# One square per batch on ScalarE and one sum on VectorE for the Frobenius norms of the converted gradients

## What is computed

```python
def _zeropower_ns5(G):
    X = G.astype(jnp.bfloat16)
    ...
    nrm = jnp.linalg.norm(X.astype(jnp.float32).reshape(X.shape[0], -1), axis=1)
    X = X / (nrm[:, None, None].astype(jnp.bfloat16) + 1e-07)
    for a, b, c in NS_COEFFS:
        A = X @ jnp.swapaxes(X, 1, 2)
        Bm = b * A + c * (A @ A)
        X = a * X + Bm @ X
```

## Time and profile before

| what | value |
|---|---|
| time, median of 3 runs | 716.71 us (711.73, 716.71, 719.69) |
| the profiled execution's own time | 712.38 us |
| its span, first to last instruction | 710.6 us |
| mean granted clock of TensorE over it | 0.983 of full |
| busy share PE, DVE, ACT, POOL | 94%, 68%, 49%, 30% |

### The profile page before, as it was taken

One profiled execution on the slowest core, in us unless ns is written; L12 is line 12 of the kernel. 1 busy time (PEld: TensorE's weight loads), 2 busy tenths in 40 slices (PEclk: granted clock), 3 DMA queues, 4 the chain that ended last, 5 costly groups with the idle time before them and its releaser, 6 DMA issues.

```text
span 710.6 us, 11547 instructions
## 1 busy us (share of the span) xinstructions
PE 665.6 (94%) x4132; PEld 568.1 (80%) x4132; DVE 483.3 (68%) x960; ACT 345.2 (49%) x746; POOL 212.3 (30%) x210
## 2 busy tenths in 40 slices
PE   3998889779997899998999999999999999999997
PEld 3778779779995688887888888888888888888885
DVE  4788888999995478767545675665754766655555
ACT  3367669879998976453322323323223223223222
POOL 2255867944037664134100330013200331000000
PEclk9999999999998899999999999999999999999999
DMA  8000000021000000032003432243212432121223
GB/s 315 1 0 1 2 1 1 1 68 48 3 3 2 0 1 1 0 118 92 30 15 83 118 104 72 63 108 112 85 60 76 117 118 69 60 69 59 66 72 122
DMA packets 20472, 41.48 MB, mean 58 GB/s; under 512 B 3360, under 2 KB 3616, under 8 KB 20288
## 3 DMA queue, kind: packets, MB, share of 16 engines
q1 hardware_dynamic: 19392, 37.65, 17.2%
q10 hardware_dynamic: 832, 2.43, 1.0%
q0 software_dynamic: 192, 0.66, 0.2%
HBM read 38.50 MB, written 2.23 MB: 57 GB/s over the span
## 4 chain that ended last, share of the span: by engine, by line
PE 73%; ACT 9%; DVE 9%; POOL 3%; issue 3%; DMA 2%; ACTq 0%; DVEq 0%; POOLq 0%
PE ps L987 36%; PE ps L1058 18%; ACT junk L634 3%; PE ps L804 3%; PE ps L917 2%; PE ps L893 2%; PE ps L918 2%; PE ps L904 2%; PE ps L933 2%; DMA qkvw<-in_qkvw 1%; PE ps L834 1%; ACT junk L586 1%; PE ps L1005 1%; PE ps L1024 1%; DVE sq L1172 1%
## 5 line engine op out<-in xcount | busy, mean ns | idle before, releaser
L705 ACT ACTIVATE sgm<-ps,zero 128x512 f32<-128x512 f32 x100 | 68.9, 690 | 268.7 <-PE ps L987 268.7
L987 PE MATMUL ps<-h2hi,whi 128*128 128x512 f32 x400 | 156.1, 390 | 0.0
L987 PE MATMUL ps<-h2lo,whi 128*128 128x512 f32 x400 | 155.6, 389 | 0.0
L987 PE MATMUL ps<-h2hi,wlo 128*128 128x512 f32 x400 | 155.6, 389 | 0.0
L1466 DVE TENSOR_TENSOR am<-sgm,ps 128x512 f32<-128x512 f32 x88 | 60.6, 688 | 138.6 <-ACT sgm L705 138.5
L449 POOL CAST whi<-raw 128x768 fp32r<-128x768 f32 x25 | 22.4, 895 | 239.2 <-DMA raw<-in_moew 236.7
L987 PEld LDWEIGHTS ps<-h2lo,whi 128*128 128x128 f32 x400 | 75.1, 188 | 15.7
L987 PEld LDWEIGHTS ps<-h2hi,whi 128*128 128x128 f32 x400 | 75.1, 188 | 15.5
L987 PEld LDWEIGHTS ps<-h2hi,wlo 128*128 128x128 f32 x400 | 75.1, 188 | 15.4
L1058 PE MATMUL ps<-ahi,whi 128*128 128x512 f32 x200 | 77.9, 390 | 0.1
L1058 PE MATMUL ps<-alo,whi 128*128 128x512 f32 x200 | 77.8, 389 | 0.0
(11 more groups left out here) (206 smaller groups left out, 1238.5 us busy)
## 6 DMA issues: line engine op xcount, KB each, us to landing
raw<-in_moew SPq DMA_DIRECT2D x25, 384.0 KB, 3.8
cw<-combine SPq DMA_DIRECT2D x32, 256.0 KB, 3.2
cw<-combine SPq DMA_DIRECT2D x16, 224.0 KB, 3.0
cw<-combine SPq DMA_DIRECT2D x16, 192.0 KB, 2.9
cw<-combine SPq DMA_DIRECT2D x16, 160.0 KB, 2.7
cw<-combine SPq DMA_DIRECT2D x16, 128.0 KB, 3.0
out<-x1T SPq DMA_DIRECT2D x8, 256.0 KB, 3.7
cw<-combine SPq DMA_DIRECT2D x16, 96.0 KB, 2.8
```

Of the source, the lines that this page charges most:

```text
L705: ac.activation(sgm[:, n % 2, :], gate_bank(n), ACT.Silu, bias=zero[:, :]).then_inc(S["e_sg"], 1)
L987: last = mm(o, w_, a_[:, kc, tok], start=(kc == 0 and k == 0), stop=(kc == KC - 1 and k == 2))
```

## The change

The six activations of `grad_squares(b)` become one activation over all six matrices of the batch, 128x768 elements, without the running sum; it writes the squares to a new tile `xsq` in fp32, which lies in memory that the queries no longer need. A new DVE function `square_sums(b)` sums `xsq` along the rows into six columns of `fss`. It is called in DVE's pass b + 2 between the second `dgb` operation and `cast_grads`, for b = 0 to 5, and for b = 6 after the loop, between a copied transpose and `x_init(3)`. The semaphore `f_sq` says that the squares are there; `f_ss` now counts batches. Batch 7 is treated as before.

```diff
@@ memory and semaphores
         X = at("X", [P, NMAT, P], BF16, R_q)
+        xsq = at("xsq", [P, 6, P], F32, R_q + NMAT * P * 2)
...
-            "xb_ok", "f_ss", "g_sq", "f_s7",
+            "xb_ok", "f_sq", "f_ss", "g_sq", "f_s7",
@@ ScalarE
             def grad_squares(b):
                 ac.wait_ge(S["xb_ok"], b + 1)
-                for m in range(b * 6, b * 6 + 6):
-                    if m:
-                        ac.wait_ge(S["f_ss"], m)
-                    ac.activation(junk[:, :], X[:, m, :], ACT.Square, bias=zero[:, :], accum_out=fss[:, m:m + 1]).then_inc(S["f_ss"], 1)
+                if b:
+                    ac.wait_ge(S["f_ss"], b)
+                ac.activation(xsq[:, :, :], X[:, b * 6:b * 6 + 6, :], ACT.Square, bias=zero[:, :]).then_inc(S["f_sq"], 1)
@@ TensorE
             def frob_sums(b):
                 if b < B - 1:
-                    pe_.wait_ge(S["f_ss"], 6 * (b + 1))
+                    pe_.wait_ge(S["f_ss"], b + 1)
@@ VectorE
+            def square_sums(b):
+                ve.wait_ge(S["f_sq"], b + 1)
+                ve.tensor_reduce(fss[:, 6 * b:6 * b + 6], xsq[:, :, :], AX.X, ALU.add).then_inc(S["f_ss"], 1)
+
             for b in range(B):
...
                 ve.tensor_tensor(dgb[i][:, :, :], dgb[i][:, :, :], dh_ps(i), ALU.mult).then_inc(S["b_dg"], 1)
+                if b >= 2:
+                    square_sums(b - 2)
                 if b >= 1:
                     cast_grads(b - 1)
                 if b >= 5:
                     x_init(b - 5)
             first_turned(1)
+            square_sums(B - 2)
             x_init(B - 5)
             x_init(B - 4)
             x_init(B - 3)
```

## The result

The changed kernel takes 719.58 us (median of 20 runs, 715.12 to 722.31), the kernel before, measured beside it, 714.69 us (median of 20 runs, 709.70 to 719.69). The ratio is 1.0067 with a 95% interval of 1.0049 to 1.0086: slower by 4.8 us (3.5 to 6.1). The profiled execution took 720.61 us, its span 718.8.

A forecast was written before the change was run, and what follows sets the result against it. The prediction took PE and ACT as full in the gradient passes, with DVE close and leading into the rounds. 3.7 us to the first `Br` plus 0.6 for the clock gave +4.3 on 716.71: 721.0 us, range 715.5 to 726.0.

The forecast's parts named there:

- The sign and the size: Whole kernel: slower by 4.3 us, 0.6%, to 721.0 us; chance 0.55.
- What bounds the passes: Gradient passes: PE is full, so the 2.2 us a pass that ACT gives back only turns into waiting.
- The prices: New instructions: ACT's square of 128x768 takes 0.93 us, DVE's sum of 128x768 takes 0.953 us.
- DVE up to its last gradient operation: Passes 3 to 7: DVE's sums partly fill idle time, leaving the second `dgb` of pass 7 1.21 us late.
- The hand-over: Into the Newton-Schulz rounds: new waits make transposes 2.35 us later, `x_init(3)` 4.4 and the first `Br` 3.7.
- The clock: PE behind its second gap, 3.0 us long: the clock may fall, costing +0.6 us, bounds 0 and 1.4.
- That sums and GpSimd get in each other's way: Rival, passes 5 to 7: sums stretch by 0.5 us each beside GpSimd, +5.8 us, 722.5 us; chance 0.08.
- a net gain from ACT: Rival, gradient passes: DVE's sums stay hidden and ACT's relief counts, 715.7 us; chance 0.08.
- The last hand-over costs less: Rival, into the rounds: ACT is free earlier or DVE has unseen slack, about +2 us, 718.7 us; chance 0.16.
- A slowdown of over 1% by the clock: Rival, PE between 135 and 155 us: low clock stretches follow one another, +7.2 us, 723.9 us; chance 0.13.

The follow-up runs named there:

- The kernel without the hand-over's waits: Changed kernel, PE's batch 5 sum over partitions behind first transposes in another PSUM bank, DVE's batch 6 sum between two divisions: 47.09 us to `Br`, ratio 1.0040.
- the two that moved one of them each: Changed kernel with DVE's batch 6 sum behind three divisions, 47.94 us to `Br`; or PE's batch 5 sum over partitions behind first transposes, 48.42 us.
- the kernel whose first gap was filled: Changed kernel with 64 unused identity products on PE ahead of batch 5's sum over partitions: 48.05 us to `Br`, ratio 1.0038.

## Why the prediction was right, point by point

- **The sign and the size.** Forecast were +4.3 us, 0.6%; measured +4.8 (3.5 to 6.1), 0.67%. The predicted 721.0 us is 1.4 over the measured 719.58, since it was added to a median of three runs, 716.71, which twenty runs put at 714.69. The profiles account for 3.6 us, and for 0.9 more in one of two executions; what may be left up to 4.8 lies inside the interval, and no stretch shows it.
- **What bounds the passes.** Right in the main: taking 1.9 us a pass from ACT is worth 0.66 us in all. But the prediction put it at nothing, by reading PE's busy 5.83 of 5.88 us as full, and the pass without the sums took 5.53. A second thing was missed. PE waits for DVE's sums in the early passes too, 0.35 to 0.38 us each for batches 0, 2 and 3, besides the 1.40 for batch 4; the first made pass 3 0.25 us longer, of which pass 4 gave 0.12 back.
- **The prices.** ACT's square 0.93 us forecast, 0.927 measured; DVE's sum 0.953 forecast, 0.944 measured.
- **DVE up to its last gradient operation.** +1.21 forecast, +0.98 measured, and not by the forecast's steps: DVE was 0.23 us late by pass 4 already, where the forecast had nothing, behind PE's wait for the sum of batch 0. The sums do fill the idle time ahead of the casts. Further on, DVE's instructions beside GpSimd's took other times than before: the cast of pass 6 took 0.98 us for 0.55, `x_init(1)` 1.15 for 1.36, and the second gate operation of passes 6 and 7 0.69 for 0.97 and 0.96.
- **The hand-over.** The transposes +2.35 forecast and +2.36 measured, `x_init(3)` +4.4 and +4.40, `Br` +3.7 and +3.60. The first is right partly by luck: DVE was 0.2 us less late, and PE's sum over partitions, for which I took 0.27 us, took 0.42 in the slow clock. The kernel without the hand-over's waits (47.09) shows that the mechanism is the one named; the two that moved one of them each won less than expected.
- **The clock.** +0.6 forecast, between 0 and 1.4. It was +0.88 in one profile and nothing in the other; that a value between them came near the measured time is luck. The step that was off is the length of PE's second gap, 3.0 us forecast and 2.15 and 1.43 measured. PE came out of its first gap in the slow clock, which lasted some 6.8 us and not the 3.45 of before; the gradient products of batch 7 took 4.5 and 5.2 us, 3.9 before, and filled part of the second gap. With these products at 2.9 us, in the kernel whose first gap was filled, the second gap was 2.87.
- **The rivals.** That sums and GpSimd get in each other's way is out: 0.94 to 0.95 us for all seven. So is a net gain from ACT: the rival priced the relief at 0.96 us, alone it is worth 0.66, and DVE's sums cost more. "The last hand-over costs less" is what the kernel with the better order does, and it needed three edits. A slowdown of over 1% by the clock didn't come: neither of the changed kernel's two profiles had more than one low stretch behind the second gap.

## What to carry to other kernels

Work moved off an engine gains only what that engine's own waits let through; before moving it, look at which engines are full in the same passes (a busy share of 99% can still hide stalls, as PE's did here), and whether the one that receives it leads into the next stage. Where an engine's list has no idle time left, an instruction costs its slot, and where it also waits for another engine, everything behind it in the list waits too; of 3.60 us here, 1.69 were such waits, and moving three things in the order took them away. When one chain is shortened, follow the one that runs beside it before writing down the gain: two of the experiments fell short for that reason, one of them in part by the clock.

## What the runs showed of the hardware

PE waited for the first `Br` in ten of the twelve profiles. The wait was 1.39 to 1.43 us in seven, the kernel before among them, and there the granted clock stayed at 1.00, with rounds of 60.34 to 60.43 us. It was 1.65, 2.15 and 2.87 us in three, and behind each the clock fell to 0.50, the 1.2 GHz level, for about 3.4 us, with rounds of 61.29 to 61.32. Such a fall took 1.7 us of PE's work and cost 0.9 us, less than the 1.4 that I had as its bound, since waits of PE fell away beside it: at full clock it waited 0.60 us for ACT's copied transpose there, in the slow clock not at all. In the changed kernel:

```profile
150.90:153.08 2.18, 0.03 (x1) 0.00 (x1) 2.15 (x5) 0.00 (x0) 0.31 (x1) 1.00 0.20 79
153.50:156.90 3.40, 3.40 (x33) 3.18 (x31) 2.22 (x5) 2.56 (x6) 0.64 (x1) 0.50 0.00 0
```

That is what this one place shows, and the length of a wait is no rule for it. Elsewhere in the same traces the clock stayed at 1.00 behind a wait of 5.06 us (the changed kernel, the first line here) and fell 1.5 us behind one of 1.34 us (the kernel before, the second line). At the same instructions of the kernel with the better hand-over PE waited 1.28 us, and no fall came:

```profile
18.90:22.90 4.00, 4.00 (x12) 3.42 (x13) 3.55 (x17) 0.16 (x1) 3.19 (x3) 1.00 0.00 0
45.30:48.30 3.00, 3.00 (x10) 2.49 (x9) 2.93 (x10) 1.66 (x3) 1.87 (x4) 0.50 0.01 3
```

Nor does the same code fall at the same time: in the first gap of the changed kernel, 4.01 and 4.02 us long, the clock fell about 2.2 us after PE's last product in one execution and about 3.6 in the other. The Trainium skill, in "TensorE: Matmul & The Clock Gate" under Why this matters for your kernels, warns of idle gaps from about 3 us up between bursts of products; the waits of 3.26 us in the kernel with the better hand-over and of 4.01 and 4.02 us in the changed one fit that, but falls also came behind 1.65 and 1.34 us, and none behind 5.06.

The second thing is how closely such a stage repeats: 48.78 and 48.81 us in two executions whose whole times were 720.61 and 718.80, so that a change of 0.1% can be read in a stretch where ten or twenty whole runs don't show it.
